# Six picked tiles in place of seven in the second layer of a graph network kernel

## What is computed

```
h = relu(layernorm(x))                       # [12500, 32]
m = relu(h[src] + edge_attr_32)              # [400000, 32]: a row of h for every edge
x = x + (1 + eps) * h + segment_sum(m, dst)  # sums by destination
```

## Time and profile before

| what | value |
|---|---|
| median of 3 runs | 7443.95 us (7433.59 to 7458.75) |
| span of the profiled execution | 7360.0 us |
| between the span and that median | 84 us |
| TensorE busy | 6429.2 us, 87% |
| GpSimd busy | 4564.4 us, 62% |
| ScalarE busy | 4370.5 us, 59% |
| VectorE busy | 3791.4 us, 52% |
| layer 1's loop, about | 3925 us to 7335 us of the span |

### The profile page before, as it was taken

The page is one execution under the profiler, slowest core; times in us unless marked ns, Lnnn a source line. Parts: engine busy times, 40 slices in busy tenths (PEclk is TensorE's granted clock), DMA queues, the critical chain, the costliest instruction groups (busy, mean ns, idle before and its releaser), DMA issues. The chain is left out here.

```text
span 7360.0 us, 107042 instructions
## 1 busy us (share of the span) xinstructions
PE 6429.2 (87%) x32834; PEld 5436.7 (74%) x32835; DVE 3791.4 (52%) x9052; ACT 4370.5 (59%) x8707; POOL 4564.4 (62%) x4834
## 2 busy tenths in 40 slices
PE   7888888888888888888887888888888889888888
PEld 5777777777777777777777777777777777777777
DVE  5343434434444443434446666666666666666666
ACT  5555555555555555555556666666666666666665
POOL 5666666666666666666655666666666666666665
PEclk8999899888898999898998999999999999999999
DMA  3222221222222122222211111111111111111111
GB/s 104 55 55 55 54 54 54 55 55 55 55 56 54 54 55 55 54 54 57 56 44 43 42 44 44 44 39 44 44 42 41 44 44 42 41 44 44 44 39 40
DMA packets 331462, 367.43 MB, mean 50 GB/s; under 512 B 87161, under 2 KB 256536, under 8 KB 331166
## 3 DMA queue, kind: packets, MB, share of 16 engines
q0 software_dynamic: 152000, 160.05, 10.0%
q1 hardware_dynamic: 46276, 130.67, 5.3%
q10 hardware_dynamic: 133146, 76.25, 3.7%
HBM read 358.17 MB, written 8.46 MB: 50 GB/s over the span
## 5 line engine op out<-in xcount | busy, mean ns | idle before, releaser
L1015 PE MATMUL bank<-part_high,owner_hot 125*128 125x448 f32 (+1 forms) x10500 | 4250.6, 405 | 224.1 <-issue 162.9
L1015 PE MATMUL bank<-part_low,owner_hot 125*128 125x448 f32 (+1 forms) x10500 | 4127.5, 393 | 152.6 <-issue 150.9
L986 POOL DMA_INDIRECT gathered<-projected_rows,indices x2500 | 2366.8, 947 | 1412.8 <-issue 705.7
L986 POOL DMA_INDIRECT gathered<-hidden_rows,indices x2250 | 2135.2, 949 | 1277.1 <-issue 854.6
L1015 PEld LDWEIGHTS bank<-part_high,owner_hot 125*128 125x128 f32 x10500 | 2144.2, 204 | 505.2 <-issue 228.8
L1015 PEld LDWEIGHTS bank<-part_low,owner_hot 125*128 125x128 f32 x10500 | 2137.9, 204 | 412.6 <-issue 189.7
L1118 ACT ACTIVATE owner_hot<-owner_in,minus_piece 125x256 fp32r<-125x256 f32 (+2 forms) x3948 | 1591.4, 484 | 128.4 <-remote 69.9
L1261 DVE SCALAR_TENSOR_TENSOR hidden<-window_f,places_now,bank 128x512 f32<-128x512 f32 x1500 | 1104.8, 737 | 1074.6 <-remote 609.0
L1123 ACT ACTIVATE owner_hot<-owner_hot 125x1792 fp32r<-125x1792 f32 (+1 forms) x750 | 1275.5, 1701 | 23.8
L1317 DVE TENSOR_TENSOR sums<-sums,bank 97x48 f32 (+1 forms) x1250 | 244.2, 195 | 1694.6 <-remote 1396.7
L1045 PEld LDWEIGHTS bank<-hidden,messages 128*97 128x97 f32 x6250 | 644.4, 170 | 424.2 <-issue 418.3
(11 more groups left out here) (128 smaller groups left out, 2721.4 us busy)
## 6 DMA issues: line engine op xcount, KB each, us to landing
owner_in<-owner_rows SPq DMA_DIRECT2D x188, 448.0 KB
edges<-in_edge ACTq DMA_DIRECT2D x124, 400.0 KB
gathered<-projected_rows,indices POOLq DMA_INDIRECT x2500
gathered<-hidden_rows,indices POOLq DMA_INDIRECT x2250
hidden<-owner_rows SPq DMA_DIRECT2D x62, 448.0 KB
edges<-in_edge ACTq DMA_DIRECT2D x124, 200.0 KB
projected_rows<-projected SPq DMA_DIRECT2D x25, 168.0 KB
sources<-in_src_cols SPq DMA_DIRECT2D x1, 1562.5 KB, 6.4
```

The lines of the kernel that those rows point to most:

```text
L986: pool.indirect_dma_start(gathered_rows(k, row)[:, t, :], None, table, bass.IndirectOffsetOnAxis(ap=index(k, odd(turn))[:, t:t + 1], axis= ...
L1015: last = nc.tensor.matmul(bank[pick_home[home]][:, 0:PITCH * D].rearrange("p (f b) -> p f b", b=PITCH)[:, :, 0:rows.shape[2]], pick_hot(pi ...
```

## The change

Layer 1 leaves out the pick with row 5: the second picked tile of chunk 4 (slot 3, tile 3). That tile is now gathered by GpSimd with the other three of its chunk. The list of banks has 12 entries in place of 14, two iterations of six picks. Everything else follows from the table's length. Layer 0 stays as it is, and the row-5 line of the owner rows is still computed and loaded.

```
 LAYER_PICKS = ((tuple(pick for pick in PICK_TABLE if pick.tile == TILES - 1),) * 2,
-               (PICK_TABLE, PICK_TABLE))
+               (tuple(pick for pick in PICK_TABLE if pick.row != 5),) * 2)
...
                 LOOK, SELECT = 2, 1
-                pick_home = [0, 1, 2, 5, 6, 0, 1, 2, 5, 6, 0, 1, 2, 5]
+                pick_home = [0, 1, 2, 5, 6, 0, 1, 2, 5, 6, 0, 1]
                 ROW_BANK = 7
```

## The result

The change makes the kernel **slower by 1.8%**: 7577.96 us (median of 4 runs, 7573.85 to 7582.92) against 7447.64 us (4 runs) for the kernel before in the same comparison, a ratio of 1.0182 with a 95% interval of 1.017 to 1.0195. That is 130 us more where 254 us less were predicted, and outside the range. One and the same kernel ran at two levels 1% apart, the kernel before at medians of 7350 to 7352 us in some comparisons and of 7422 to 7448 us in others, and its profile (span 7360.0 us) is of the quicker level, that of the change of the slower one.

What follows compares the result with a forecast made beforehand. The prediction took TensorE to bound the kernel. One pick less (-369 us), one gather more (+40) and the bank list (+75) summed to -254 us, a 7106 us span, with 84 us added 7190 us; range 7020 to 7370 us.

Steps and rivals of the forecast that it cites:

- One gather more on GpSimd: Layer 1, GpSimd's 19th gather: mostly hidden behind TensorE, +0.3 us an iteration, +40 us; bounds 0 and +4.2 us an iteration.
- signs of being wrong: Layer 1: clock under 0.90, GpSimd waiting over 3 us, or a 23.7 us iteration with GpSimd never waiting would disprove steps.
- the first reading: Layer 1: TensorE bounds the 27.2 us iteration, with 22.0 us of work and 5.2 us of bursts and low clock.
- One pick less: TensorE, layer 1: 14 matmuls and weight loads leave each iteration, 2.95 us, -369 us; bounds -456 and 0.
- VectorE and ScalarE: Layer 1: VectorE loses one select, about 1.4 us, ScalarE's second batch has two rows, not three; costed at nothing.
- The list of banks: At the 12-entry list's wrap, two picks wait for VectorE's place: 0.6 us an iteration, +75 us; bounds 0 and +231 us.
- The rule that speaks against the change: TensorE in layer 1: cycling through PSUM banks makes its clock swing, so new bank waits would lower it; 7428 us.
- The fourth: Rival: GpSimd becomes the bound and keeps all its waiting, at line 984; 28.5 us an iteration, 7606 us, chance 0.08.
- The third: Rival on TensorE's clock: new waits double the share at 1.2 GHz, 1.9 us an iteration, 7428 us, chance 0.06.
- The 84 us around the span: Whole kernel: the run median exceeds the profiled 7360.0 us span by 84 us, carried along into the forecast time.

Runs made afterwards that it cites:

- e1: The change with the same five banks reordered so none is used again before four picks later; 7485.9 us, 1.0185 of the kernel before.
- e3: The change with both the reordered banks of e1 and the added gather left out (six picks, 18 gathers); 7324.7 us, ratio 0.9966 to the kernel before.
- e7: The change with two gathers an iteration left out, in chunks 4 and 2 (six picks, 17 gathers); 7253.64 us, ratio 0.9756 to the kernel before.
- e2: The change with its added gather left out, stale rows instead (six picks, 18 gathers); 7330.29 us, ratio 0.9973 to the kernel before.
- e4: The kernel before, seven picks, with one more gather in chunk 4 into memory nobody reads (19 gathers); 7521.07 us, ratio 1.0231.
- e14: The kernel before's seven picks with only two gathers a chunk in layer 1, ten an iteration; 6721.92 us, ratio 0.9143 to the kernel before.
- e13: The change, six picks, with only two gathers a chunk in layer 1, ten an iteration; 6357.57 us, ratio 0.8649 to the kernel before.
- e6: The change with 7 of the 14 products of each layer 1 pick, low halves left out; 7490.19 us, ratio 1.0076 to the kernel before.
- e16: The kernel before changed the other way: eight picks, 17 gathers, second picks in chunks 1, 3 and 5; 7292.4 us, ratio 0.982.
- e10: The change without GpSimd's wait for picks in the middle of a chunk in layer 1; 7607.81 us, ratio 1.022 to the kernel before.
- e12: The kernel before without GpSimd's wait for picks in the middle of a chunk in layer 1; 7468.94 us, ratio 1.0033.
- e5: The change with both of GpSimd's waits for TensorE's picks removed in layer 1; 8051.39 us, ratio 1.084 to the kernel before.
- e9: e5 with two stops GpSimd makes itself each iteration, in chunks 2 and 4, independent of TensorE; 7642.47 us, ratio 1.0274 to the kernel before.
- e11: The change, waits for picks kept, with the two added GpSimd stops of e9; 7624.86 us, ratio 1.0238 to the kernel before.
- e8: The kernel before with both of GpSimd's waits for TensorE's picks removed in layer 1; 8008.8 us, ratio 1.0772.

## Why the prediction was wrong

**The step that failed** is "One gather more on GpSimd": "I take +0.3 us, near the lower end, because a lagging GpSimd finds its semaphores already raised." The iteration is 28.7 us in the change's profile and 28.3 us in e1's, 4.0 to 4.4 us over the 24.3 us that the step took as TensorE's need, where it had 0.3; that is its upper bound of 4.2. GpSimd's waiting stayed (4.6 to 5.0 us, 4.8 before). The added gather costs 1.29 to 1.36 us an iteration (e1 against e3, e7 against e2, e4), not 0.3. Two of the prediction's own signs of being wrong were there: GpSimd waiting over 3 us, and a clock under 0.90.

**Behind it stands the first reading**, that TensorE bounds the kernel. The prediction had the number that speaks against it: seven picks and five scatters make 22.0 us, and e14 runs at 22.1. It put the other 5.2 us of the 27.2 down to TensorE's own bursts and clock (2.9 and 1.8 us of them). With gathers out of the way both vanish (clock 1.00, next to no idle time), so they were slack. GpSimd had 22.5 us of gathers and 4.8 us of waiting. Two engines with nearly the same work, 22.0 and 22.5 us, each with some 5 us left over: the prediction took the one remainder as belonging to the work and the other as room, and it was the other way round. TensorE's 87% busy and its 40% of the chain did not show the bound.

**One pick less** (-369 us): the price was right, 2.91 us in e14 against e13 and 2.95 predicted, and not to be had here: 20 us in e2. The stated upper bound, "0, where another engine takes the time", was all but the case.

**VectorE and ScalarE**, costed at nothing: nothing in the runs speaks against it.

**The list of banks** (+75 us): the waits came, 125.0 us in 3150 us, 1.1 us an iteration where 0.6 was expected. They cost nothing that can be measured: 1.0182 with them, 1.0185 without (e1).

**The rule that speaks against the change:** the clock did fall, 0.93 to 0.88, and new bank waits did appear. If they had made it fall, e1, which removes them, should have given it back; its clock in layer 1 is 0.87 and its time the same. So no run here shows that the bank waits made the clock fall. It is 0.70 in e6, where TensorE idles most, and 1.00 in e13, e14 and e16, where it idles least. The Trainium skill, "TensorE: Matmul & The Clock Gate", section "A second HAM failure mode: psum-queue depth-cycling", has the clock swing in a kernel that cycles through PSUM banks.

**The rivals.** The fourth, given 0.08, is what happened, in mechanism and nearly in size: 162 us more were worked out, 130 us measured. Its ground, that semaphores "come late from TensorE whatever its lag", is what the delays show. The place that it named, the wait at line 984, is not where the time goes: without that wait the kernels are 0.3 to 0.4% slower (e10, e12). The ground held against it, "a later arrival at the same semaphore waits less", fails because the signal does not come at a time of its own: it mostly comes once GpSimd has stopped. The third's 1.9 us for a doubled share of the lower clock is 1.8 by the prediction's own figure, which moves 7428 by some 12 us and no chance.

**The 84 us around the span** are none: the change's profiled execution spans 7572.1 us and took 7573.85 us. They were the distance between two executions of the kernel before, and stand in 7444 as in 7190, so the -254 us don't hang on them.

**What stays open.** That long runs of gathers go with late signals, and that stops let them pass, is shown by e5, e9, e11, e13 and e14 and by the recorded raises. The recorded raises also account for additions that start within a burst, 19% before and 25% in the change, at least in part: a raise due at the first gathers of a burst mostly passes at once. By which way gathers hold a TensorE signal back inside the chip is not shown. That the pauses must come to some 4.9 us an iteration is a fit over 17 to 19 gathers; e13 and e14 run outside it. A kernel with all 18 or 19 gathers and a short stop after every two or three of them was not run, nor was a stream of 19 gathers with no dependence on the loop's own data.

## What to carry to other kernels

Where two engines that exchange work each wait for the other, neither busy share nor the chain tells whose waits are room. Get each engine's own pace from a run in which the other's work is cut, as e13 and e14 do here for TensorE, before an instruction moves from one to the other, and price the move once with the receiver's waits kept whole. Then test both directions: the gain of 1.8% lay in the other one.

## What the runs showed of the hardware that I had not expected

- A TensorE signal reaches VectorE 0.13 to 0.14 us after the end of the matmul with ten gathers an iteration, and 5.7 to 6.9 us after it (medians of those waited for) with 18 or 19. TensorE's raises go out on time for 84 to 92% of those due at the first gather of a burst and for 1% from the sixth on, and come out in order, five within 0.31 us in the case shown. VectorE's and ScalarE's raises are at 0.008 to 0.012 us throughout.
- Taking all waits for TensorE out of GpSimd's loop makes the kernel 7.7 to 8.4% slower (e8, e5). Here a wait that paces GpSimd is what lets TensorE's signals through.
- A gather keeps its 0.95 us and the 0.30 us to the next one in every run with 17 to 19 gathers; what differs from run to run is where the pauses lie, and how long they are (2.3 to 2.9 us in the mean, 3.2 in e6, over 5 in e5 and e8).
- Halving the matmuls of every pick takes the granted clock to 0.70 in layer 1, and the kernel is still 1% quicker than the change at 0.88.
